# A three-hop graph layer with LayerNorm on one core: the mean leaves the row statistics and goes into the weights, and squares are summed for four tiles at once

## The reference, cut to what matters

```python
def _spmm(src, dst, w, feats, n):                    # 25,000 edges, 100,000 nodes
    return segment_sum(w[:, None] * feats[src], dst, num_segments=n)
feats, cur = [x], x                                  # x: 100000 x 256, f32
for _ in range(3):
    cur = _spmm(src, dst, edge_weight, cur, 100000)
    feats.append(cur)
y = x + concatenate(feats, 1) @ shared_weight + output_bias      # 1024 x 256, 256
m, v = mean(y, -1), var(y, -1)
return (y - m) / sqrt(v + 1e-5)
```

## Time and profile before

| | |
|---|---|
| Time, median of 3 runs | 1551.88 us (1550.68 to 1554.51) |
| Profiled execution, its own time | 1555.48 us |
| Its span, first to last instruction | 1553.7 us |
| Busy: PE, DVE, ACT, POOL | 92%, 78%, 69%, 69% of the span |
| Mean granted TensorE clock | 0.967 |
| DMA | 410.75 MB, mean 264 GB/s |

### The profile page before, as it was taken

How to read it: one execution, slowest core, us unless ns; L and a number is a source line. 1 busy time by engine, 2 the same in 40 slices (tenths; PEclk the granted TensorE clock), 3 DMA queues, 4 the chain that set the end, 5 groups by cost and what they waited for, 6 DMA issues and landing times. The chain is left out here.

```text
span 1553.7 us, 30950 instructions
## 1 busy us (share of the span) xinstructions
PE 1423.4 (92%) x7990; PEld 1219.7 (79%) x7990; DVE 1206.0 (78%) x4923; ACT 1076.9 (69%) x2674; POOL 1070.8 (69%) x1047
## 2 busy tenths in 40 slices
PE   7999999999999996699979989999898888989994
PEld 5888888888888875578868878877777776877883
DVE  6877777777777778978754766459999999998774
ACT  4777777777777752368865655647878787878775
POOL 4577777777777755747746777854777777777734
PEclk9999999999999999799999999999999999999997
DMA  8888888888888875379975887779999999999862
GB/s 261 251 270 270 277 282 275 280 267 274 280 282 280 267 218 172 101 256 321 320 253 159 238 242 210 201 192 307 338 327 325 322 337 332 329 315 340 294 202 109
DMA packets 214375, 410.75 MB, mean 264 GB/s; under 512 B 31044, under 2 KB 137533, under 8 KB 214202
## 3 DMA queue, kind: packets, MB, share of 16 engines
q1 hardware_dynamic: 164582, 311.03, 59.0%
q0 software_dynamic: 48624, 97.04, 22.3%
q10 hardware_dynamic: 996, 0.72, 0.2%
HBM read 227.02 MB, written 194.09 MB: 271 GB/s over the span
## 5 line engine op out<-in xcount | busy, mean ns | idle before, releaser
L1488 PE MATMUL ps_y<-w_sb,xT 128*128 128x256 f32 (+1 forms) x1928 | 506.1, 392 | 11.8 <-DVE y_ring L1845 9.2
L1199 ACT ACTIVATE o_ring<-y_ring,shift,rstd 128x256 f32<-128x256 f32 (+1 forms) x782 | 422.2, 589 | 0.0
L1488 PEld LDWEIGHTS ps_y<-w_sb,xT 128*128 128x128 f32 (+1 forms) x1928 | 356.0, 197 | 54.0 <-issue 7.7
L1845 DVE TENSOR_TENSOR y_ring<-ps_y,bias 128x512 f32<-128x512 f32 (+1 forms) x325 | 224.0, 689 | 141.2 <-PE ps_y L1488 127.9
L1851 DVE BATCH_NORM_STATS2 stats<-y_ring 128x6 f32<-128x256 f32 (+1 forms) x782 | 291.2, 414 | 4.2
L919 POOL DMA_INDIRECT rows_in<-in_x,gather_idx x200 | 201.3, 1006 | 87.2 <-issue 70.3
L919 POOL DMA_INDIRECT tails_found<-tail_keys,table_idx x200 | 200.3, 1001 | 81.1 <-issue 59.0
L923 POOL DMA_INDIRECT out_rows<-u_out,early_node x173 | 178.2, 1030 | 83.0 <-issue 43.5
L919 POOL DMA_INDIRECT rows_in<-out_rows,early_node x160 | 166.7, 1042 | 80.3 <-issue 40.5
L1573 PE MATMUL ps_u<-w_sb,cT 128*128 128x256 f32 x788 | 206.2, 384 | 0.0
L1477 PE MATMUL ps_xT<-ident,x_ring 128*128 128x128 f32 x1140 | 178.1, 280 | 15.2 <-ACT xT L1186 9.0
(11 more groups left out here) (364 smaller groups left out, 2648.1 us busy)
## 6 DMA issues: line engine op xcount, KB each, us to landing
x_ring<-in_x SPq DMA_DIRECT2D x195, 512.0 KB, 6.6
out_rows<-o_ring SPq DMA_DIRECT2D x195, 512.0 KB, 4.0
c_rows<-sums SPq DMA_DIRECT2D x49, 512.0 KB
u_rows<-u_out SPq DMA_DIRECT2D x49, 512.0 KB, 4.8
keys_bc<-u_rows SPq DMA_DIRECT2D x21, 512.0 KB, 7.1
listed<-u_rows SPq DMA_DIRECT2D x14, 512.0 KB, 6.5
c_list_rows<-sums SPq DMA_DIRECT2D x11, 512.0 KB
u_out<-c_list_rows SPq DMA_DIRECT2D x44, 128.0 KB, 5.4
```

The costliest lines, as they stand in the source:

```text
L1199: last = act.activation(o_ring[slot][0:rows, r * D:(r + 1) * D], y_ring[k][0:rows, r * D:(r + 1) * D], ACT.Identity, bias=shift[k][0:rows, ...
L1488: last = pe.matmul(y_bank[p][0:rows, r * D:(r + 1) * D], columns_in[p][:, q * P:q * P + rows], w_sb[:, c, :], start=c == 0, stop=c == KC - 1)
L1845: dve.tensor_tensor(y_ring[k][0:rows, half * 2 * D:(half + 1) * 2 * D], y_bank[p][0:rows, :], bias2[0:rows, :], ALU.add).then_inc(y_copied, 1)
```

## The change

The weight matrix (with the identity added to its first block) and the bias are centred once: from each row of the weights its mean over the 256 outputs is subtracted, in `centre_weights`, and likewise from the bias. A row's mean is then zero but for rounding, so the shift goes, and the variance is the mean of the squares. From the six statistics the sum of squares of a row is 128 * mean^2 of each half plus count by variance of each half: one scalar_tensor_tensor squares the eight half means of four tiles in place, and one reduce adds the sixteen numbers, for four tiles at once. ACT divides by 256 in the root's scale and normalises with Copy and a scale alone. Between squares and sums stands a wait (`squared`, `csquared`). The sparse late tile at the end keeps its bn_aggr, but not its shift.

```diff
 def roots(u, k, rows=P, tiles=RPP):
-    act.activation(std_all[...], mean_var[k][0:rows, 0:tiles, 1], ACT.Sqrt, bias=eps[0:rows, :]).then_inc(std_ready, 1)
+    act.activation(std_all[...], squares[k][0:rows, 0:tiles], ACT.Sqrt,
+                   scale=1.0 / D, bias=eps[0:rows, :]).then_inc(std_ready, 1)
 def normalise(u, k, slot, turn, half, rows=P):
-        act.wait_ge(shift_ready, u + 1)
+        act.wait_ge(rstd_ready, u + 1)
...
-                              ACT.Identity, bias=shift[k][0:rows, r:r + 1],
-                              scale=rstd[k][0:rows, r:r + 1])
+                              ACT.Copy, scale=rstd[k][0:rows, r:r + 1])
 def multiply_u(e):
-        pe.wait_ge(weights_loaded, 16)
+        pe.wait_ge(weights_ready, 5)
-def unit_variance(k, rows=P, tiles=RPP):
-    for r in range(tiles):
-        last = dve.bn_aggr(mean_var[k][0:rows, r, :], stats[k][0:rows, r, :])
-    last.then_inc(var_ready, 1)
-def unit_shift(u, k, rows=P, tiles=RPP):
...
+def unit_squares(k, rows=P, tiles=RPP):
+    means = stats[k][0:rows, 0:tiles, :].rearrange("p r (h f) -> p r h f", f=3)[:, :, :, 1]
+    dve.scalar_tensor_tensor(out=means, in0=means, scalar=float(D // 2), in1=means, op0=ALU.mult,
+                             op1=ALU.mult).then_inc(squared, 1)
+def unit_variance(u, k, rows=P, tiles=RPP):
+    dve.wait_ge(squared, u + 1)
+    parts = stats[k][0:rows, 0:tiles, :].rearrange("p r (h f) -> p r h f", f=3)[:, :, :, 1:3]
+    dve.reduce_sum(squares[k][0:rows, 0:tiles], parts, mybir.AxisListType.XY).then_inc(var_ready, 1)
 def unit_end(u, k):
     dve.wait_ge(stats_ready, 2 * u + 2)
+    unit_squares(k)
     unit_inverse(u - 1, (k - 1) % STEP)
-    unit_variance(k)
-    unit_shift(u - 1, (k - 1) % STEP)
+    unit_variance(u, k)
...
+def centre_weights(first, end, ready):
+    dve.wait_ge(rows_summed, ready)
+    dve.reduce_sum(row_sums[:, first:end], w_sb[:, first:end, :], mybir.AxisListType.X).then_inc(rows_summed, 1)
+    dve.wait_ge(rows_summed, ready + 1)
+    return dve.scalar_tensor_tensor(out=w_sb[:, first:end, :], scalar=-1.0 / D, in1=w_sb[:, first:end, :],
+                                    in0=row_sums[:, first:end].unsqueeze(2).broadcast_to([P, end - first, D]),
+                                    op0=ALU.mult, op1=ALU.add)
+centre_weights(0, KC, KC).then_inc(w0_ready, KC)
 dve.wait_ge(bias_loaded, 32)
+dve.reduce_sum(bias_sum[:, :], bias2[:, 0:D], mybir.AxisListType.X).then_inc(w0_ready, 1)
+dve.wait_ge(w0_ready, KC + 1)
+dve.scalar_tensor_tensor(out=bias2[:, :], in0=bias_sum[:, :].broadcast_to([P, 2 * D]), scalar=-1.0 / D,
+                         in1=bias2[:, :], op0=ALU.mult, op1=ALU.add).then_inc(w0_ready, 1)
...
 # stage A, first step
+                        if q == 0:
+                            dve.wait_ge(weights_loaded, 16)
+                            centre_weights(KC, BLOCKS * KC, KC + 1).then_inc(weights_ready, 1)
                         find_own(q)
...
 # stage D, def step_d (group_squares and group_variance are the unit's two steps, for four edge tiles)
-                    if measured:
+                    if measured and (q % G == 2 or n == REAL + 2):
                         dve.wait_ge(cstats_ready, n - 2)
+                        group_squares((n - 3) // G, (n - 3) % G + 1)
...
-                    if measured:
-                        c_aggregate((q - 3) % Q, ...)
+                    if measured and (q % G == 2 or n == REAL + 2):
+                        group_variance((n - 3) // G, (n - 3) % G + 1)
                     if q % G == 3 and ...:
                         c_inverse(g - 1, 1 - half)
-                        c_shift(g - 1, 1 - half)
...
 # the late tile
-                dve.reciprocal(lrstd[:, :], lstd[:, :]).then_inc(late_chain, 1)
                 dve.wait_ge(late_out, 16 * j + 16)
                 columns(lateo_idx[:, :], late_node, t, 1)
-                dve.wait_ge(late_chain, 4 * j + 4)
-                dve.scalar_tensor_tensor(out=lshift[:, :], in0=lmv[:, 0:1], scalar=-1.0, in1=lrstd[:, :], ...)
+                dve.reciprocal(lrstd[:, :], lstd[:, :]).then_inc(late_chain, 1)
```

More of the change, by code:

```diff
@@ L157, in gnn_program @@
         stats = [sb(f"stats{k}", [P, RPP, 6]) for k in range(STEP)]
-        mean_var = [sb(f"mean_var{k}", [P, RPP, 2]) for k in range(STEP)]
+        squares = [sb(f"squares{k}", [P, RPP]) for k in range(STEP)]
+        row_sums = sb("row_sums", [P, BLOCKS * KC])
+        bias_sum = sb("bias_sum", [P, 1])
         std_all = sb("std_all", [P, RPP * (UNITS + 1)])
         rstd = [sb(f"rstd{k}", [P, RPP]) for k in range(STEP)]
-        shift = [sb(f"shift{k}", [P, RPP]) for k in range(STEP)]
         rows_in = [sb(f"rows_in{k}", [P, D]) for k in range(Q)]
@@ L1189, in roots @@
                 act.wait_ge(var_ready, u + 1)
-                act.activation(std_all[0:rows, RPP * u:RPP * u + tiles], mean_var[k][0:rows, 0:tiles, 1], ACT.Sqrt,
-                               bias=eps[0:rows, :]).then_inc(std_ready, 1)
+                act.activation(std_all[0:rows, RPP * u:RPP * u + tiles], squares[k][0:rows, 0:tiles], ACT.Sqrt,
+                               scale=1.0 / D, bias=eps[0:rows, :]).then_inc(std_ready, 1)
             def normalise(u, k, slot, turn, half, rows=P):
                 if half == 0:
-                    act.wait_ge(shift_ready, u + 1)
+                    act.wait_ge(rstd_ready, u + 1)
                     until(act, stored[slot], 16 * turn)
@@ L1403, in c_roots @@
                 act.wait_ge(cvar_ready, g + 1)
-                act.activation(cstd[half][:, :], cmv[half][:, :, 1], ACT.Sqrt, bias=eps[:, :]).then_inc(cstd_ready, 1)
+                act.activation(cstd[half][:, :], csquares[half][:, :], ACT.Sqrt, scale=1.0 / D, bias=eps[:, :]).then_inc(cstd_ready, 1)
             def c_normalise(n, q, group, turn):
-                act.wait_ge(cshift_ready, group + 1)
+                act.wait_ge(crstd_ready, group + 1)
                 if q % 2 == 0:
@@ L1410, in c_normalise @@
                 half, k = q // G, q % G
-                act.activation(co[q], cy[q], ACT.Identity, bias=cshift[half][:, k:k + 1],
-                               scale=crstd[half][:, k:k + 1]).then_inc(cnormed, 1)
+                act.activation(co[q], cy[q], ACT.Copy, scale=crstd[half][:, k:k + 1]).then_inc(cnormed, 1)
             def step_d(d, slot=None):
@@ L2702, in c_inverse @@
                 dve.reciprocal(crstd[half][:, :], cstd[half][:, :]).then_inc(crstd_ready, 1)
-            def c_shift(g, half):
-                dve.wait_ge(crstd_ready, g + 1)
-                dve.scalar_tensor_tensor(out=cshift[half][:, :], in0=cmv[half][:, :, 0], scalar=-1.0, in1=crstd[half][:, :],
-                                         op0=ALU.mult, op1=ALU.mult).then_inc(cshift_ready, 1)
             def step_d(d, par, turn, copies=None, measures=None):
```

73 lines of the change are left out of this document (30 added, 43 removed).

## The result

The changed kernel takes 1543.56 us (median of 6 runs, 1542.91 to 1546.68), the kernel before 1553.2 us beside it (6 runs, 1549.18 to 1555.53). The ratio of the runs is 0.9949, interval 0.9935 to 0.9963: faster beyond the noise, though by half a percent only, 7.9 us (5.7 to 10.1) of 1551.88. (The two medians alone are 9.6 us apart, which lies in the same interval.) The prediction said 1537, a gain of 14.9 us. The time lies in its range, 1527 to 1550, but its likeliest case forecast nearly twice the gain. The profiled execution after took 1543.65 us, with a span of 1541.6.

What follows compares the result with a forecast made beforehand. DVE, 98.2% busy, was taken to set D's pace, with POOL and DMA nearly full; PE bounds A. D 13, C 0.7, end 1, list 1, start -0.8 sum to 14.9 us off: 1537 us, range 1527 to 1550.

Steps and rivals of the forecast that it cites:

- its likeliest case: Whole kernel: 14.9 us off, 1537 us against the median of 1551.88; chance 0.48.
- A unit's end: DVE in D, from squares to the next instruction: 0.25 to 0.35 us instead of 0.41, gain taken as 0.08 us.
- the strided reduce: DVE's reduce over two strided axes, sixteen numbers, absent from the old trace: taken as 0.08 us, bounded by 0.05 and 0.61.
- The slower rival: In D the reduce over two axes is slow, turning the sign at 0.26 us: 1568 us; chance 0.06.
- I take 13 us, the DMA's lower ceiling less a little: D's sixteen steps: DVE offers 17.6 us, the DMA's lower ceiling is 14 us, so 13 us arrive.
- its 9 us of waits and 11 us of slip: POOL in D can lose 9 us of waits and slip about four slots, 11 us: a ceiling near 20 us.
- nearly full neighbours don't yield: In D POOL can't slip or the DMA saturates: some 6 us there, 8 in all, 1544 us; chance 0.24.
- Everything yields: In D POOL's indirect DMAs shorten, freeing 9 us, and DVE's 24 us arrive: 1527 us; chance 0.10.
- So PE comes 1.1 us late, less what two or three cheaper unit ends give back: 0.8 us: Start of stage A: 3.5 us of centring on DVE, mostly covered, delays PE by 0.8 us net.
- Without the cover it is 3.5 us: Start of stage A: if no idle time hides the centring of the six other blocks, the loss is 3.5 us.
- 1 us in the list and 0.7 in C: Cheaper DVE unit ends gain 1 us in the list (560 to 700 us); lighter ACT normalisations gain 0.7 us in C.
- the 1 us forecast: End of the kernel: lighter ACT normalisations in the last chain, with the late tile's shift gone, gain 1 us.

Runs made afterwards that it cites:

- the run with two operands: Changed kernel, but every normalisation on ACT uses Identity with a second per-partition operand, a column of zeros: 1547.35 us, ratio 0.9971 to the kernel before.

## Why the prediction was half right

**What DVE saves: right.** A unit's end takes 0.32 us (0.25 to 0.35 forecast), the strided reduce 0.08 to 0.11 (0.08 taken). DVE is busy for 339.86 of 350 us, for a step 0.971 * 21.07 = 20.46 us, against 343.87/350 * 21.91 = 21.52: a saving of 1.06 us where 1.1 was forecast. The slower rival's reduce of 0.26 us did not appear.

**"I take 13 us, the DMA's lower ceiling less a little": the number by `row_std` is right, the reason and the place where it was read are wrong.** The sixteen steps gained 13.4 us at `row_std`, but only 10.6 us at the first turned edge tile. The runs show in its place that POOL is the ceiling. Its list from D's first `row_std` to its first gather of `tail_node` was shortened by 7.4 us: 1406.4 - 1051.7 = 354.7 before, 1397.4 - 1050.1 = 347.3 after. Forecast was room for 20 us, its 9 us of waits and 11 us of slip. The slip is real, 6.0 us of it (POOL's first gather of `tail_node` starts 10.2 us behind the last `row_std`, before 4.2), but it is a loan: at the hand-over PE waits 3.3 us for it. I had priced the end of D at nothing, since from 1402 us on PE is the bound. That is true only if the first gather of that stage comes as early as DVE does. The rival "nearly full neighbours don't yield" said that POOL would go from DMA to DMA with 0.30 us between, and it does; its reason, a landing that frees ACT's buffer, is how POOL's pace reaches DVE, though POOL did slip. That its time, 1544 us, was met is partly luck: it had 6 us in D, where 10.6 came, and 0.8 us of loss at the start, where 5.2 went. "Everything yields" had POOL's DMAs shorten as DVE grows lighter: in the changed kernel they took 1.046 us as before.

**"So PE comes 1.1 us late, less what two or three cheaper unit ends give back: 0.8 us": wrong, it is 5.2 us.** I followed one chain out of DVE's list, the one to `own_r`, found 2.5 us of cover on it, and did not follow the other instruction that was queued behind the passes: the squares of a dense unit. Through ACT's root and the carry's copy behind it, they hold PE itself, which waits 3.61 us. And the cover was none: the 1.70 us that DVE stood idle were a wait for PE, and since PE is late too, DVE stands there for 3.76 us now; the 0.7 us between DVE's last instruction and PE's turn of `own_r` are 0.8 now. The wait is 2.9 of the 5.2 us, the other 2.3 come behind it, for the most part with the lower clock, a term that the prediction did not have. "Without the cover it is 3.5 us" was nearer, and lacked the clock. Moving two thirds of the passes away returned 4.7 us of the 5.2 in the trace, doubling them added 3.7.

**The smaller terms.** ACT's normalisation takes 498 ns, 506 forecast:

```profile
L1199 ACT ACTIVATE o_ring<-y_ring,rstd 128x256 f32<-128x256 f32 (+1 forms) x782 | 350.1, 498 | 0.0
```

That is 91 ns less; the Trainium skill (ScalarE: Activation LUTs, What ACT_TABLE_LOAD costs) has 93, nearer than my 83. Forecast were 1 us in the list and 0.7 in C. A, list, B and C together gained 4.2 us from `own_r` on, by one trace of each kernel; how much of it is ACT's, DVE's or chance is open. I had counted B at nothing. The end gained 1.3 us from the last turned edge tile on (1526.9 to 1553.7 before, 1516.1 to 1541.6 after), 0.9 of it through ACT by the run with two operands, against the 1 us forecast, but PE lost 1.4 us ahead of it, behind the wait at the hand-over (112.3 us from the first to the last turned tile, 110.9 before).

**The sum.** Forecast 13 + 0.7 + 1 + 1 - 0.8 = 14.9. Measured in the same places 10.6 + 4.2 - 5.2 - 0.1 = 9.5, and 7.9 us by the ratio. Of the 5.4 us between them 4.4 are the start, 2.4 are D with the hand-over and 1.1 the end, against which A to C stand 2.5 better. The 1.6 us between the traces and the ratio are inside its interval.

## What to carry to other kernels

When an engine that is 98% busy is relieved, add up the next one's list with its gaps between instructions: 248 us busy of 328 looked like 76%, and with 0.30 us between 237 DMAs it was 97%. The prediction did that sum, and then gave POOL 11 us of slip without a price. Follow the gain to the first place where another stage takes over from the saturated engine, since a lead that came out of its slack is paid back there. When work is put into an engine's list, go through every instruction queued behind it and its readers on other engines, not only through the chain that one has in mind; early in this program most of such a delay reached the end (4.7 us moved away in the trace, 3.9 gained by the ratio).

## What the runs showed of the hardware

In D the indirect DMAs take POOL 1.02 to 1.07 us each in these runs, and 0.306 us lie between two of them even with a register instruction less. Small DVE instructions of 0.13 to 0.18 us mostly start 0.05 to 0.12 us apart in the rows of both kernels, a reduce over two strided axes of 16 numbers among them. The DMA engines were at a share of 1.00 with 357 GB/s. Around PE's wait of 3.6 us in the first step of A its granted clock fell to the lower level for some microseconds (0.57 from 36 to 42 us), in one execution later and for less long (0.72); where the wait was 1.43 us it stayed at 1.00. With two scatters less the last scatter of the profiled run ended the span 10 us after its start, where it was 5 in the changed kernel. I did not look into it; that profiled execution was the slowest of its four.
